# A two-layer graph network on one core: first layer's VectorE instructions in another order, part of the one-hot tiles of the weighting on ScalarE

## The reference, cut to what matters

```python
# layer 0, for each edge e (src -> dst)
msg = table_src[src] + table_dst[dst]              # two gathers, one sum
m1  = tensor_product(msg, y[e], rbf[e] @ W_rbf)    # products, dots, cross products
a   = sum(leaky_relu(m1_s @ W_alpha) * alpha_dot)  # 4 heads
ex  = exp(a - segment_max(a, dst)[dst])
val = (m1 @ W_val), vectors times sigmoid(val_s @ Wg), scalars through sigmoid
h   = tensor_product(val, y[e], w2) @ W_vlin
agg = segment_sum(ex * h, dst) / segment_sum(ex, dst)
# layer 1, for each edge e
w   = silu(edge64[e] @ fc_w1) @ fc_w2
mid = tensor_product(hid_table[src], y[e], w)
agg = segment_sum(mid, dst)        # then linear maps, sigmoid gates, the sum with x
```

## Time and profile before

| | us |
|---|---|
| median of 3 runs (lowest, highest) | 4113.28 (4111.42, 4117.14) |
| the profiled execution, its own time | 4107.93 |
| its span | 4106.1 |
| layer 0's edges, about | 147 to 2420 |
| segment maximum, about | 2420 to 2476 |
| weighting, about | 2476 to 2752 |
| layer 1's edges, about | 2939 to 4045 |

### The profile page before, as it was taken

One profiled execution on the slowest core, in us unless ns is written; L12 is line 12 of the kernel. 1 busy time (PEld: TensorE's weight loads), 2 busy tenths in 40 slices (PEclk: granted clock), 3 DMA queues, 4 the chain that ended last, 5 costly groups with the idle time before them and its releaser, 6 DMA issues. The chain is left out here.

```text
span 4106.1 us, 96246 instructions
## 1 busy us (share of the span) xinstructions
PE 3645.6 (89%) x21340; PEld 2699.0 (66%) x21340; DVE 3743.4 (91%) x13030; ACT 2873.1 (70%) x10728; POOL 2644.8 (64%) x2464
## 2 busy tenths in 40 slices
PE   3799999999999999999999967875799999999997
PEld 2588888888888888888888856863333333333335
DVE  6599999999999999999999988976599999999995
ACT  0488888888888888888888852111377777777775
POOL 0577777777777777777777731110377777777772
PEclk9999999999999999999999988995699999999999
DMA  5333333333333333333333318980233333333333
GB/s 157 94 88 89 88 89 87 88 88 87 89 88 89 87 88 88 87 89 88 89 87 88 88 47 243 259 231 6 63 94 94 93 95 95 93 95 92 94 94 114
DMA packets 299250, 410.92 MB, mean 100 GB/s; under 512 B 98196, under 2 KB 234388, under 8 KB 298932
## 3 DMA queue, kind: packets, MB, share of 16 engines
q0 software_dynamic: 127008, 208.99, 22.0%
q1 hardware_dynamic: 172180, 201.26, 15.2%
HBM read 309.09 MB, written 100.94 MB: 100 GB/s over the span
## 5 line engine op out<-in xcount | busy, mean ns | idle before, releaser
L720 POOL DMA_INDIRECT SC<-dst_tab,idx x784 | 963.6, 1229 | 239.5 <-issue 234.0
L784 POOL DMA_INDIRECT ACC<-hid_tab,idx x784 | 818.9, 1045 | 416.4 <-issue 237.4
L709 POOL DMA_INDIRECT ACC<-src_tab,idx x784 | 768.1, 980 | 427.6 <-issue 246.2
L1048 ACT ACTIVATE MT<-TR 128x768 f32<-128x768 f32 x784 | 593.8, 811 | 5.7 <-PE TR L834 5.7
L834 PE MATMUL TR<-ident,M 128*128 128x128 f32 x4704 | 579.6, 273 | 7.5 <-DVE M L1359 7.2
L1037 ACT ACTIVATE ACC<-W,ACC 128x64 f32<-128x64 f32 x2352 | 583.3, 344 | 0.0
L834 PEld LDWEIGHTS TR<-ident,M 128*128 128x128 f32 x4704 | 527.8, 141 | 8.8 <-DVE M L1359 8.3
L883 PE MATMUL HP<-w_hv,MT 128*128 128x128 f32 x3136 | 520.0, 288 | 0.0
L858 PE MATMUL E<-w_mv,MT 128*128 128x128 f32 x3136 | 477.2, 275 | 0.0
L858 PEld LDWEIGHTS E<-w_mv,MT 128*128 128x128 f32 x3136 | 437.0, 191 | 0.0
L826 PE MATMUL W<-w_rbf,rbf 16*128 16x224 f32 x1568 | 402.0, 375 | 20.3 <-DMA rbf<-in_rbf_line 18.2
(11 more groups left out here) (242 smaller groups left out, 7812.7 us busy)
## 6 DMA issues: line engine op xcount, KB each, us to landing
h_tab<-ACC SPq DMA_DIRECT2D x392, 160.0 KB, 1.8
SC<-h_tab SPq DMA_DIRECT2D x50, 640.0 KB, 5.2
TAB<-h_tab SPq DMA_DIRECT2D x48, 640.0 KB, 5.3
ACC<-in_e64T SPq DMA_DIRECT2D x98, 256.0 KB
ACC<-src_tab,idx POOLq DMA_INDIRECT x784
SC<-dst_tab,idx POOLq DMA_INDIRECT x784
ACC<-hid_tab,idx POOLq DMA_INDIRECT x784, 3.7
agg_tab<-ACC POOLq DMA_DIRECT2D x49, 240.0 KB
```

The source lines that it names most:

```text
L709: pool.indirect_dma_start(gat0[:, v.slot8, g, :], None, src_tab.ap(), bass.IndirectOffsetOnAxis(ap=idx[:, v.sslot, c:c + 1], axis=0))\
L720: pool.indirect_dma_start(gatd[:, v.slot8, g, :], None, dst_tab.ap(), bass.IndirectOffsetOnAxis(ap=idx[:, v.sslot, c:c + 1], axis=0))\
L784: pool.indirect_dma_start(gat1[:, v.slot8, g, :], None, hid_tab.ap(), bass.IndirectOffsetOnAxis(ap=idx[:, v.sslot, c:c + 1], axis=0))\
L1048: nc.scalar.activation(dst[:, 0:3].rearrange("p k g e -> p (k g e)"), tr[:, 0:3 * G, :].rearrange("p a e -> p (a e)"), ACT.Copy).then_inc( ...
```

## The change

First layer, DVE: `products0` now returns after its first product (L1341) and is called ahead of `scaled`; the next product (L1342, `crossed0`) stands between `scaled` and `mixed`; the other two (L1343, L1344, `others0`) stay where `products0` stood. No instruction is added or taken away there; `products0`'s waits (for the factors of chunk t + 1, for `m`, for the transposes of two chunks before) move forward with it.

Weighting: DVE makes five of the eight one-hot tiles. ACT makes the last three (`NA = 3`): three activations Square(place - iota) of 128 columns, each with a per-partition bias, then, after a wait for them, one Relu(1 - x) of 384 columns into the tile buffer. ACT's loop starts one step earlier. PE has one more wait (`oha`).

`locate`: the window's first node is now subtracted from all 784 columns of `dst` at once, in the segment-maximum stage (one instruction); the weighting and layer 1 read `dstf` at a place computed at run time in every step, and L1536 is gone from both.

```diff
+            def one_hots_a(v, total):            # ACT
+                if v.wide:
+                    act.wait_ge(LC["loc"], v.sup + 1)
...
+                if v.past(1):
+                    act.wait_ge(LC["oha"], v.num)
+                    act.sem_inc(s_passed, 1)
+                for i in range(NA):
+                    k = 2 * Q * (v.place + 1) - NA + i
+                    c = v.data() * (2 * Q1) + k
...
+                    place = loc1[:, v.sslot, k:k + 1] if v.wide else dstf[:, bass.ds(c, 1)]
+                    ins = nc.scalar.activation(far[:, i, :], iota[:, :], ACT.Square, bias=place, scale=-1.0)
+                ins.then_inc(LC["far"], 1)
+                if v.past(2):
+                    act.wait_ge(LC["sc"], v.num - 1)
+                    act.sem_inc(s_passed, 1)
+                act.wait_ge(LC["far"], v.num + 1)
+                act.sem_inc(s_passed, 1)
+                nc.scalar.activation(ohC[:, v.par, 2 * Q - NA:2 * Q], far, ACT.Relu, bias=onec[:, 0:1], scale=-1.0)\
+                    .then_inc(LC["oha"], 1)
...
             def stage_c(t, total):
                 ones_c(t, total)
+                one_hots_a(t + 1, total)
                 take_sums(t + -1, total)
-            both(act, lambda sups, wide: loop_steps(act, 2, sups, wide, 0, 1, stage_c))
+            both(act, lambda sups, wide: loop_steps(act, 2, sups, wide, 1, 1, stage_c))
...
                 done = summed(t + -1, total, ups)
+                parts = products0(t + 1, total, added)
                 scaled(t + -1, total, done)
+                crossed0(t + 1, total, parts)
                 mixes = mixed(t + -1, total)
                 mixed_sums(t + -1, total, mixes)
                 up = head_products(t + -2, total)
-                parts = products0(t + 1, total, added)
+                crosses = others0(t + 1, total, parts)
                 head_values(t + -2, total, up)
...
+                places_all = dstf[:, :].rearrange("p (s k) -> p s k", s=NS1)
+                ch.count(TT(places_all, places_all, ax(nbase[:, :], (1, NS1), (0, 2 * Q1)), ALU.add))
...
-                if v.place == 0:
-                    locate(v)
+                locate(v)                        # now only for v.wide
                 if v.past(2):
                     dve.wait_ge(LC["sc"], v.num - 1)
-                lo = 2 * Q * v.place
-                TT(ohC[:, v.par], ax(iota[:, 0:1], (0, 2 * Q), (1, P)), ax(loc1[:, v.sslot, lo:lo + 1], (1, 2 * Q), (0, P)),
+                n = 2 * Q - NA
+                TT(ohC[:, v.par, 0:n], ax(iota[:, 0:1], (0, n), (1, P)), places_of(v, 2 * Q * v.place, n),
                    ALU.is_equal).then_inc(LC["oh"], 1)
...
-                TT(ohE[:, v.slot], ax(places[:, 0:1], (0, G), (1, P)),
-                   ax(loc1[:, v.sslot, 2 * v.place:2 * v.place + 1], (1, G), (0, P)), ALU.is_equal).then_inc(LB["oh"], 1)
+                TT(ohE[:, v.slot], ax(places[:, 0:1], (0, G), (1, P)), places_of(v, 2 * v.place, G),
+                   ALU.is_equal).then_inc(LB["oh"], 1)
```

More of the change, by code:

```diff
@@ L37 @@
 AR = NP + P
+NA = 3
 Q1 = 2 * Q
@@ L226, in program @@
         agC = flat[:, 4672:4672 + 2 * HF].rearrange("p (b f) -> p b f", b=2)
+        far = flat[:, 11600:11600 + NA * P].rearrange("p (i f) -> p i f", i=NA)
         exC = sb("exC", [P, 4, 8 * H])
@@ L404, in program @@
         LC = dict(ld=[sem(f"c_ld{u}") for u in range(4)], add=[sem(f"c_add{u}") for u in range(2)],
-                  **{k: sem(f"c_{k}") for k in ("oh", "one", "hx", "sc", "ev")})
+                  **{k: sem(f"c_{k}") for k in ("oh", "loc", "far", "oha", "one", "hx", "sc", "ev")})
         LB = dict(ld=[sem(f"b_ld{u}") for u in range(2)], ix=[sem(f"b_ix{u}") for u in range(2)],
@@ L921, in sums_c @@
                 pe.wait_ge(LC["oh"], v.num + 1)
+                pe.wait_ge(LC["oha"], v.num + 1)
                 pe.wait_ge(LC["hx"], v.num + 1)
@@ L1126, in ones_c @@
                                      ax(exC[:, v.slot, 0:1], (H, 8), (0, 3), (1, H)), ACT.Copy).then_inc(LC["one"], 1)
+            def one_hots_a(v, total):
+                if not inside(v, total):
+                    return
+                if v.wide:
[7 more added lines that the diff above has]
+                    c = v.data() * (2 * Q1) + k
+                    c = c if v.base is None else c.with_bounds(min_val=k, max_val=NC - 2 * Q1 + k)
+                    place = loc1[:, v.sslot, k:k + 1] if v.wide else dstf[:, bass.ds(c, 1)]
[5 more added lines that the diff above has]
+                act.wait_ge(LC["far"], v.num + 1)
+                act.sem_inc(s_passed, 1)
+                nc.scalar.activation(ohC[:, v.par, 2 * Q - NA:2 * Q], far, ACT.Relu, bias=onec[:, 0:1], scale=-1.0)\
+                    .then_inc(LC["oha"], 1)
             def take_sums(v, total):
@@ L1339, in mid, with crossed0, others0 @@
                     return ax(Mt[:, 0, lo:lo + 1], (MW, G), *dims)
[L1341 to L1345, removed]
+                return mid, feat, wgt, ch.count(TT(mid(0, (C, 3), (1, C)), feat(S, (C, 3), (1, C)), wgt(160, (64, 3), (1, C)),
+                                                   ALU.mult))
+            def crossed0(v, total, parts):
+                if parts:
+                    mid, feat, wgt, dots = parts
+                    TT(fX[:, :, 0:2, 0, :], feat(S, (C, 2), (1, C)), wgt(192 + 64, (64, 2), (1, C)), ALU.mult)
+            def others0(v, total, parts):
+                if parts:
+                    mid, feat, wgt, dots = parts
+                    TT(fX[:, :, 0:2, 1, :], feat(S + C, (C, 2), (1, C)), wgt(192, (64, 2), (1, C)), ALU.mult)
+                    return ch.count(TT(fX[:, :, 2], feat(S + 2 * C, (-2 * C, 2), (1, C)), wgt(192, (128, 2), (1, C)), ALU.mult))
             def rest_of_s0(v, total, parts):
                 if parts:
-                    mid, feat, wgt, dots, crosses = parts
+                    mid, feat, wgt, dots = parts
                     ch.wait(dots)
@@ L1352, in rest_of_s0, with rest_of_v0 @@
                     TT(mid(96, (S, 2), (1, S)), feat(0, (0, 2), (1, S)), wgt(C, (S, 2), (1, S)), ALU.mult)
-            def rest_of_v0(v, total, parts):
+            def rest_of_v0(v, total, parts, crosses):
                 if parts:
-                    mid, feat, wgt, dots, crosses = parts
+                    mid, feat, wgt, dots = parts
                     ch.wait(crosses)
@@ L1453, in stage0 @@
                 up = head_products(t + -2, total)
[L1454 removed]
+                crosses = others0(t + 1, total, parts)
                 head_values(t + -2, total, up)
                 rest_of_s0(t + 1, total, parts)
[L1457 removed]
+                rest_of_v0(t + 1, total, parts, crosses)
             loop_steps(dve, Q, NS, False, 1, 2, stage0)
@@ L1529, in _, with columns_of, places_of @@
                 dve.sem_inc(s_diff, 1)
+            def columns_of(v, k, n):
+                first = v.data() * (2 * Q1) + k
+                return bass.ds(first if v.base is None else first.with_bounds(min_val=k, max_val=NC - 2 * Q1 + k), n)
             def locate(v):
[L1532 to L1536, removed]
+                if v.wide and v.place == 0:
+                    nb = nodecon[:, bass.ds(v.window(), 1), 1:2].rearrange("p a f -> p (a f)")
+                    ch.step(TS(loc1[:, v.sslot, :], dstf[:, columns_of(v, 0, 2 * Q1)], nb, None, ALU.add))
+                    if v.q == 2:
+                        dve.sem_inc(LC["loc"], 1)
+            def places_of(v, k, n):
+                return ax(loc1[:, v.sslot, k:k + n] if v.wide else dstf[:, columns_of(v, k, n)], (1, n), (0, P))
             def one_hots_c(v, total):
@@ L1611, in one_hots1 @@
                     return
-                if v.place == 0:
-                    locate(v)
+                locate(v)
                 if v.past(4):
                     dve.wait_ge(LB["sc"], v.num - 3)
-                TT(ohE[:, v.slot], ax(places[:, 0:1], (0, G), (1, P)),
-                   ax(loc1[:, v.sslot, 2 * v.place:2 * v.place + 1], (1, G), (0, P)), ALU.is_equal).then_inc(LB["oh"], 1)
+                TT(ohE[:, v.slot], ax(places[:, 0:1], (0, G), (1, P)), places_of(v, 2 * v.place, G),
+                   ALU.is_equal).then_inc(LB["oh"], 1)
             def products1(v, total):
```

## The result

The changed kernel takes 4086.9 us (median of 4, 4081.7 to 4092.6), the kernel before 4112.4 beside it: ratio 0.9936, interval 0.9919 to 0.9953, so 26 us faster (19 to 33). Forecast were 4082 and 31 us less.

The account below looks back on a forecast made before the run. Layer 0 was taken as bound by a circle through PE and ACT, the weighting by DVE, layer 1 by POOL. Weighting -27, layer 0 -5, subtraction +1 give -31 us: median 4113.3 becomes 4082, range 4058 to 4102.

Parts of the forecast that it names:

- a circle through PE and ACT: Layer 0: e1, L1370, sigmoids, ACT's copy, hm on PE set the 5.77 us step; the new DVE order does not shorten it.
- DVE's share of layer 0 at about 91%: Layer 0, a sign to look for: DVE's busy share falls from 96% to about 91%.
- The 5 us at the loop's end: Layer 0: every eighth step DVE delays the circle by about 0.1 us; the new order hides it, 49 x 0.1 = 5 us.
- POOL's 5.62 as layer 0's lower bound: Layer 0: POOL's gathers let the step fall no lower than 5.62 us, at most 63 us of gain.
- Rival 1: Layer 0: DVE's order holds L1370, so the step falls to 5.62 to 5.65, another 50 us, 4032; 10%.
- The weighting, -27 us: Weighting: the step falls from 2.74 to 2.45 us, set by a circle through two buffers; 93 steps give 27 us.
- 4.90 for a pair: Weighting: the circle through two buffers takes 2.55 + 2.28 + 0.07 = 4.90 us for two steps, 2.45 a step.
- the 2.6 above which the prediction would have called itself wrong: Weighting: the prediction declared itself wrong if the step came out above 2.6 us.
- rival 2: Weighting: the transfers, at DMA share 0.94, hold the step at 2.58 us; 15 us instead of 27, 4094; 14%.
- rival 3: Weighting: Square or Relu is not in Exp's table, so ACT pays two 1.283 us loads a step, 4319; 4%.
- Layer 1, 0 (bounds 0 and 8): Layer 1: dropping L1536 saves DVE 13 us, all hidden behind POOL, so 0 us, at most 8.
- Rival 4: Layers 0 and 1: the new order (run-time places, gathers falling otherwise) costs over 30 us; 3%.

Follow-up runs that it names:

- split_old: Kernel before, layer 0's DVE order old, with ACT's copy ahead of hm cut in two: 4079.6 us against 4110.1, ratio 0.9929.
- split_new_four: Changed kernel with ACT's copy in layer 0 cut in two and four buffers instead of two in the weighting: 3911.2 us against 4110.1, ratio 0.9516.
- weighting_only: Changed kernel with layer 0's old DVE order, on a chip with stalls: 5062.9 us beside 5083.8 for the kernel before, ratio 0.9956.
- half_rows: Changed kernel with only half of each h_tab row group loaded in the weighting, all instructions kept: executed once, 4086.2 us.
- l0_order_only: Kernel before with only layer 0's new DVE order, on a chip with stalls: 5174 us against 5084, ratio 1.0156.

## Why the prediction was right, and where it was off

- *Layer 0 is held by a circle through PE and ACT, which the edit does not touch.* Right. The step stayed 5.77, L1407 starts behind `e1` with idle time before it, and the order alone gives a ratio of 0.9997. This nothing is not because a wait between neighbours on DVE is free: with the circle shortened the same order gave 112 us. Cutting ACT's copy moved the bound to DVE's 5.72, where the prediction had "about 5.70".
- *DVE's share of layer 0 at about 91%.* It is 94%. The 0.33 us by which DVE's sequence shrinks was taken off its busy time, but 0.16 of them had been idle time in the two gaps (0.13 and 0.03 by the earlier trace rows).
- *The 5 us at the loop's end.* Wrong. The two long steps in eight, 5.86 and 5.88, are there in both kernels, so DVE's 0.46 was not what made them long. In `split_old`, where DVE's sequence sets the step, they shrink to 5.71 and 5.75 beside 5.72. That speaks for a cost of the loop's end on PE or ACT; no run tells which.
- *POOL's 5.62 as layer 0's lower bound.* Wrong: 5.43 was reached, because the gathers' length is not a constant. Rival 1 fell, and was priced too low with it: going down to 5.43 is worth 141 us, not 50.
- *The weighting, -27 us.* The mechanism was right (a circle of two steps through two buffers; four buffers take it away, half the transfers change nothing) and its size off. I had 4.90 for a pair, it is 5.20: PE starts 0.34 or 0.18 behind L1606 where I took 0.07 from one row, and 2.66 pass from PE's start until DVE goes on where I took 2.55, though the row read 2.61. These two terms make 93 x 0.15 = 14 us, all of the miss. The row of 0.07 was of a step that does not open a window, and the circle runs through those that do. At every other one of these the trace of before shows 0.19 to 0.23 from L1558's end to PE's start, here 0.19:

```profile
2604.51 0.95 DVE L1558 TENSOR_TENSOR ACC<-SC,ex 128x768 f32<-128x768 f32 x1
...
2605.65 2.25 PEld L927 LDWEIGHTS HP<-ACC 128*128 128x128 f32 x16 [0.75 <-ACT ACC L1134]
```

  The step of 2.60 lies just at the 2.6 above which the prediction would have called itself wrong.
- *DMA share as a floor (rival 2).* Fell. The share rose from 0.94 to 1.00 and bounded nothing.
- *Table loads (rival 3).* Fell: the changed kernel has one load ahead of Exp and none in the weighting, as the earlier trace rows showed before.

```profile
L1118 ACT ACT_TABLE_LOAD x1 | 1.3, 1283 | 1.1 <-issue 1.1
```

  So Square and Relu are served by the set that Exp left. The Relu took 0.61 (estimate 0.5, upper end 0.8), a square 0.39 (0.57 at most).
- *Layer 1, 0 (bounds 0 and 8).* It gave 4 us in the changed kernel's profile and 10 with the places alone. POOL's gathers are the bound, as argued, but they became shorter, 1.037 and 1.030 us on average instead of 1.045; 784 x 0.008 and 0.015 are 6 and 12 us. With the 1101.4 to 1103.4 of the undisturbed runs that keep L1536, and the 1093.4 to 1099.2 of those without it, the gain is real; that DVE's work beside them is what shortens the gathers is likely, since layer 0 shows the same. Rival 4, an unfavourable turn of over 30 us in a layer, fell on these chips; on one with stalls layer 0's new order lost 90 us.
- *The subtraction over 784 columns* took 0.98 us, forecast 0.95.

Sum: measured 26 us against 31. The weighting gave 13 less than forecast and layer 0's order 5 less, which leaves 13 of the 31; layer 1 gave 4 to 10, and 3 to 9 us stand in no profile (the two profiled executions differ by 15, of which two single steps cost 5). That the sum came out so near is in part luck; the weighting's term alone was twice what it measured.

## What to carry to other kernels

Before moving an engine's work, walk once round the step, from an instruction to itself, and add what lies on the way; an instruction filled into a gap is worth something only if that way goes through the gap. Here 0.33 us a step of DVE's time was worth nothing, and 0.29 after one copy on another engine had been cut in two. Where two buffers alternate, price the circle (write, hand over, use, hand back) against the engine's own time; they can stand level, and then relieving the engine alone gives nothing. Among waits ahead of an instruction, put the one that is met last in the last place; it was worth 7 us of 258 here, and nothing once four buffers had taken the wait away.

## What the runs showed of the hardware that was not expected

- The length of POOL's indirect gathers follows what DVE does. With the same bytes and indices the destination gather averaged 1.229 us in the kernel before, 1.125 when only DVE's order was changed, 1.091 in the changed kernel and 1.041 in `split_new_four`, where DVE is busy 1795 of 1800 us; so it is not DVE's busy share alone. Single gathers go down to 0.94; in the kernel before the second destination gather of a step mostly takes 1.57. That it hangs on which instructions run beside it is argued: the old order on a chip with stalls (`weighting_only`) has 1.018, and `half_rows`, with the changed kernel's layer 0, 1.140 where that had 1.091.
- A DMA busy share of 1.00 at 274 GB/s left room for 319 GB/s in the same stage.
- On two chips the kernel before takes 5063 and 5084 us, nearly a quarter more. The weighting is the same there to 1 us; layers 0 and 1 have stalls. In `l0_order_only` (above) and its repeat on the other kind of chip (below), layer 0's stretches read:

```profile
300.00:3200.00 2900.00, 2405.91 (x14410) 2122.91 (x14409) 1975.23 (x7927) 1786.60 (x6483) 1458.59 (x1440) 0.84 0.23 63
```

```profile
300.00:2200.00 1900.00, 1810.93 (x13119) 1599.19 (x13118) 1782.75 (x7215) 1585.40 (x5903) 1401.13 (x1311) 1.00 0.33 88
```

  PE's granted clock averages 0.84 instead of 1.00 there, falling behind the stalls: in `l0_order_only` PE is busy 0.14 us between 665 and 669 us, and from 667 to 675 it is granted 0.50 (1.2 GHz). On the one of them where it was run alone, layer 0's new order loses 1.6%. Where the stalls come from, and why the new order suffers more, stays open.
